# Layer 0: the dense gate's probabilities and rank comparisons moved from VectorE to GpSimd

## The reference, cut to what matters

```python
probs = softmax(x @ Wr + br, axis=-1)                 # 8 experts
sorted_idx = argsort(-probs, axis=-1)
sorted_probs = take_along_axis(probs, sorted_idx, axis=-1)
cum = cumsum(sorted_probs, axis=-1)
mask = cum < TOP_P                                    # 0.8
mask = mask.at[..., 0].set(True)
keep = take_along_axis(mask, argsort(sorted_idx), axis=-1)
gate = probs * keep
h = relu(einsum('bth,ehf->betf', x, W1) + b1)
y = einsum('betf,efh->beth', h, W2) + b2
return einsum('bte,beth->bth', gate, y)               # all eight experts are computed
```

## Time and profile before

| | |
|---|---|
| median of three runs | 2269.92 us (2262.42 to 2271.96) |
| the profiled execution's own time | 2259.05 us |
| its span, first to last instruction | 2257.3 us |
| mean granted TensorE clock | 0.955 |
| busy share of PE, DVE, ACT, POOL | 88%, 77%, 59%, 58% |
| layer 0, from its first steady iteration to its end | from about 104 us to about 1480 us |

### The profile page before, as it was taken

One profiled execution on the slowest core, in us unless ns is written; L12 is line 12 of the kernel. 1 busy time (PEld: TensorE's weight loads), 2 busy tenths in 40 slices (PEclk: granted clock), 3 DMA queues, 4 the chain that ended last, 5 costly groups with the idle time before them and its releaser, 6 DMA issues. The chain is left out here.

```text
span 2257.3 us, 40537 instructions
## 1 busy us (share of the span) xinstructions
PE 1991.2 (88%) x13714; PEld 1149.0 (51%) x13714; DVE 1730.0 (77%) x2778; ACT 1340.6 (59%) x2421; POOL 1300.4 (58%) x975
## 2 busy tenths in 40 slices
PE   1799999999999999999999999966899999987876
PEld 0455555555555555555555555533455555544442
DVE  3498888888888888888888898845777777765555
ACT  1576776776766767767767767622445554544443
POOL 0477867767767767778677687742332333324550
PEclk9999999999999999999999999967999999998897
DMA  7615505415325235145054153242222222234337
GB/s 193 137 38 111 127 26 132 102 47 130 85 63 132 68 85 132 46 107 131 22 132 104 42 131 92 46 117 88 84 91 80 85 82 86 85 109 113 114 115 230
DMA packets 184332, 222.49 MB, mean 99 GB/s; under 512 B 28488, under 2 KB 122736, under 8 KB 180016
## 3 DMA queue, kind: packets, MB, share of 16 engines
q1 hardware_dynamic: 182064, 215.52, 37.2%
q0 software_dynamic: 2048, 4.18, 0.7%
HBM read 165.41 MB, written 54.27 MB: 97 GB/s over the span
## 5 line engine op out<-in xcount | busy, mean ns | idle before, releaser
L685 POOL TENSOR_TENSOR dBx<-REP,BC 128x1024 f32<-128x1024 f32 x256 | 603.6, 2360 | 292.7 <-DVE dA L845 246.2
L845 DVE TENSOR_TENSOR_SCAN dA<-dA,dBx 128x512 f32<-128x512 f32 x512 | 626.6, 1224 | 117.4 <-ACT dA L555 66.4
L374 PE MATMUL UP<-xnT,W 128*128 128x512 f32 x1024 | 520.4, 628 | 53.9 <-ACT hT L564 41.8
L383 PEld LDWEIGHTS DN<-W,hT 128*128 128x128 f32 x4096 | 469.4, 192 | 108.6 <-issue 98.3
L383 PE MATMUL DN<-W,hT 128*128 128x128 f32 x4096 | 496.0, 278 | 0.3 <-ACT GD L571 0.3
L564 ACT ACTIVATE hT<-UP,b 128x512 f32<-128x512 f32 x512 | 355.8, 695 | 91.6 <-PE UP L374 84.4
L555 ACT ACTIVATE dA<-REP,A 128x512 f32<-128x512 f32 x512 | 354.3, 695 | 74.3 <-DVE PR L854 73.9
L854 DVE TENSOR_TENSOR PR<-dA,BC 128x512 f32<-128x512 f32 x512 | 353.4, 690 | 31.5 <-DVE dA L845 18.8
L1748 DVE TENSOR_REDUCE NM<-S 128x4 f32<-128x1024 f32 (+1 forms) x192 | 234.2, 1220 | 135.4 <-PE S L1310 88.3
L374 PEld LDWEIGHTS UP<-xnT,W 128*128 128x128 f32 x1024 | 181.6, 196 | 282.4 <-issue 146.5
L1504 ACT ACTIVATE PT<-S 128x1024 f32<-128x1024 f32 x192 | 196.8, 1025 | 111.8 <-PE S L1332 62.4
(11 more groups left out here) (246 smaller groups left out, 2819.7 us busy)
## 6 DMA issues: line engine op xcount, KB each, us to landing
REP<-s_delta SPq DMA_DIRECT2D x128, 256.0 KB, 8.2
REP<-s_dx SPq DMA_DIRECT2D x128, 256.0 KB, 7.4
BC<-s_b SPq DMA_DIRECT2D x128, 256.0 KB, 8.6
s_parts<-SPL SPq DMA_DIRECT2D x32, 384.0 KB, 2.8
s_dx<-tz SPq DMA_DIRECT2D x16, 512.0 KB, 3.1
s_y<-zeros SPq DMA_DIRECT2D x32, 256.0 KB, 5.3
YC<-s_y SPq DMA_DIRECT2D x16, 512.0 KB, 5.1
s_delta<-soft SPq DMA_DIRECT2D x32, 255.0 KB, 2.7
```

Of the source, the lines that this page charges most:

```text
L374: nc.tensor.matmul(UP[k % 2][:], W1[:, e % E0, f * P:(f + 1) * P], xnT[:, q, :], start=True, stop=True).then_inc(upf.sem, 1)
L383: last = nc.tensor.matmul(DN[:, j * P:(j + 1) * P], hT[:, e % 2, f, j * P:(j + 1) * P], W2[:, e, f, :], start=(f == 0), stop=(f == FB - 1))
L685: nc.gpsimd.tensor_tensor(dBx[:, s % 2], DX[:, h, j:j + 2, :], BC[:, q // 2, q % 2, :].unsqueeze(1).to_broadcast([P, 2, T0]), ALU.mult).th ...
L845: nc.vector.tensor_tensor_scan(h, h, dBx[:, k // 2 % 2, k % 2, :], 0.0, ALU.mult, ALU.add).then_inc(scan_done.sem, 1)
```

## The change

GpSimd makes the probabilities and the comparisons. It computes other minus this, adds tri8, which VectorE has scaled once by 2^-126 before the loop, and compares the sum with 2^-126: a positive difference passes, a zero difference passes only with the tie term. VectorE keeps the sum, the reciprocal and the two row sums. The waits on gate_step and rank_step follow.

```diff
+TINY = 2.0 ** -126
 (GpSimd, rank, h = 24)
-                pool.wait_ge(gate_step.sem, gate_step.at(n, 7))
-                nc.gpsimd.tensor_tensor(eq[:], eq[:], tri, ALU.mult).then_inc(rank_step.sem, 1)
+                this = pr[:].unsqueeze(3).to_broadcast([P, J0, E0, E0])
+                pool.wait_ge(gate_step.sem, gate_step.at(n, 4))
+                pool.wait_ge(gate_made.sem, gate_made.at(n - 1, 5))
+                nc.gpsimd.tensor_tensor(pr[:], pe_[:], g4[:, 2, :].unsqueeze(2).to_broadcast([P, J0, E0]), ALU.mult).then_inc(rank_step.sem, 1)
                 pool.wait_ge(rank_step.sem, rank_step.at(n, 1))
-                nc.gpsimd.tensor_tensor(gt[:], gt[:], eq[:], ALU.add).then_inc(rank_step.sem, 1)
+                nc.gpsimd.tensor_tensor(eq[:], other, this, ALU.subtract).then_inc(rank_step.sem, 1)
                 pool.wait_ge(rank_step.sem, rank_step.at(n, 2))
+                nc.gpsimd.tensor_tensor(eq[:], eq[:], tri, ALU.add).then_inc(rank_step.sem, 1)
+                pool.wait_ge(rank_step.sem, rank_step.at(n, 3))
+                pool.sem_inc(paced, 1)
+                nc.gpsimd.tensor_scalar(gt[:], eq[:], TINY, None, ALU.is_ge).then_inc(rank_step.sem, 1)
+                pool.wait_ge(rank_step.sem, rank_step.at(n, 4))
                 nc.gpsimd.tensor_tensor(eq[:], gt[:], other, ALU.mult).then_inc(rank_step.sem, 1)
...
 (VectorE, once before the loop)
+        nc.vector.tensor_scalar(tri8[:], tri8[:], TINY, None, ALU.mult)
...
 (VectorE, gate1, h = 22)
-                gstep(nc.vector.reciprocal(g4[:, 2, :], g4[:, 1, :]), 4)
-                dve.wait_ge(gate_made.sem, gate_made.at(n - 1, 5))
-                gstep(nc.vector.tensor_tensor(pr[:], pe_[:], over(g4[:, 2, :]), ALU.mult), 5)
-                nc.vector.tensor_tensor(gt[:], other, this, ALU.is_gt).then_inc(gate_step.sem, 1)
-                nc.vector.tensor_tensor(eq[:], other, this, ALU.is_equal).then_inc(gate_step.sem, 1)
+                nc.vector.reciprocal(g4[:, 2, :], g4[:, 1, :]).then_inc(gate_step.sem, 1)
```

More of the change, by code:

```diff
@@ L119, in layer0 @@
     sp_done = signal("sp_done", 3); relu_done = signal("relu_done", E0 * FB); da_ready = signal("da_ready", TILES); gated = signal("gated", E0)
-    conv_step = signal("conv_step", 6); gate_step = signal("gate_step", 9); lg_done = signal("lg_done", 1); gate_made = signal("gate_made", 5); z_done = signal("z_done", 2); xi_done = signal("xi_done", 1)
+    conv_step = signal("conv_step", 6); gate_step = signal("gate_step", 6); lg_done = signal("lg_done", 1); gate_made = signal("gate_made", 5); z_done = signal("z_done", 2); xi_done = signal("xi_done", 1)
     log_step = signal("log_step", 2); delta_done = signal("delta_done", 1)
@@ L126, in layer0 @@
     xn_ready = signal("xn_ready", 4); dbx_ready = signal("dbx_ready", SLOTS); yz_done = signal("yz_done", HALF); acc_done = signal("acc_done", E0)
-    dx_done = signal("dx_done", 1); rank_step = signal("rank_step", 3); r_done = signal("r_done", 1)
+    dx_done = signal("dx_done", 1); rank_step = signal("rank_step", 5); r_done = signal("r_done", 1)
     xi_loaded = signal("xi_loaded", 16); b_stored = signal("b_stored", 16); d_stored = signal("d_stored", 16 * HALF); e_stored = signal("e_stored", 16)
@@ L766, in fore @@
                 tri = tri8[:].rearrange("p (e o) -> p e o", o=E0).unsqueeze(1).to_broadcast([P, J0, E0, E0])
-                pool.wait_ge(gate_step.sem, gate_step.at(n, 7))
-                nc.gpsimd.tensor_tensor(eq[:], eq[:], tri, ALU.mult).then_inc(rank_step.sem, 1)
+                this = pr[:].unsqueeze(3).to_broadcast([P, J0, E0, E0])
+                pool.wait_ge(gate_step.sem, gate_step.at(n, 4))
+                pool.wait_ge(gate_made.sem, gate_made.at(n - 1, 5))
+                nc.gpsimd.tensor_tensor(pr[:], pe_[:], g4[:, 2, :].unsqueeze(2).to_broadcast([P, J0, E0]), ALU.mult).then_inc(rank_step.sem, 1)
                 pool.wait_ge(rank_step.sem, rank_step.at(n, 1))
-                nc.gpsimd.tensor_tensor(gt[:], gt[:], eq[:], ALU.add).then_inc(rank_step.sem, 1)
+                nc.gpsimd.tensor_tensor(eq[:], other, this, ALU.subtract).then_inc(rank_step.sem, 1)
                 pool.wait_ge(rank_step.sem, rank_step.at(n, 2))
+                nc.gpsimd.tensor_tensor(eq[:], eq[:], tri, ALU.add).then_inc(rank_step.sem, 1)
[3 more added lines that the diff above has]
+                pool.wait_ge(rank_step.sem, rank_step.at(n, 4))
                 nc.gpsimd.tensor_tensor(eq[:], gt[:], other, ALU.mult).then_inc(rank_step.sem, 1)
             if h == POOL_AT["keep"]:
-                pool.wait_ge(gate_step.sem, gate_step.at(n, 9))
+                pool.wait_ge(gate_step.sem, gate_step.at(n, 6))
                 pool.sem_inc(paced, 1)
@@ L894, in end @@
             restatistic(it)
-        def over(v, n=E0):
-            return v.unsqueeze(2).to_broadcast([P, J0, n])
         def fore(h, n, q):
@@ L902, in gstep @@
                 dve.wait_ge(gate_step.sem, gate_step.at(n, k))
-            other = pr[:].unsqueeze(2).to_broadcast([P, J0, E0, E0])
-            this = pr[:].unsqueeze(3).to_broadcast([P, J0, E0, E0])
             for b in range(HALF):
@@ L949, in fore @@
             if h == DVE_AT["gate2"]:
-                dve.wait_ge(rank_step.sem, rank_step.at(n, 3))
+                dve.wait_ge(rank_step.sem, rank_step.at(n, 5))
                 nc.vector.tensor_reduce(cnt[:], gt[:], AX.X, ALU.add).then_inc(gate_step.sem, 1)
```

## The result

The changed kernel takes 2260.24 us, the median of 20 runs (2251.89 to 2266.7), against 2269.56 for the kernel before in 20 runs of the same session. The ratio is 0.9964, with a 95% interval of 0.995 to 0.9978: 8.2 us less, within 5 to 11. The forecast was 4 us less, and 2266 for the median.

A forecast was written before the change was run, and what follows sets the result against it. Bound: a cycle from `th` through delta and dx to the B and C load, or TensorE in other iterations. VectorE 0, GpSimd's extra 0, handover -4: 2259 to 2255 us, for a median 2269.9 to 2266; range 2248 to 2280.

The forecast's parts named there:

- VectorE's 3.19 us: VectorE's time freed per iteration around the gate, near 48 us in 15, ends as shifted idle time; gain 0.
- Rival A: VectorE is on the path after all: all 48 us would give 2222, a third 2254; chance 0.13.
- GpSimd's extra 1.18 us: GpSimd's rank step grows from 2.35 to 3.53 us an iteration, with 0.77 us for the threshold; cost 0.
- The branching rule: Data-dependent branching costs GpSimd some 12 cycles an element: threshold 2.6 us, whole rank step 5.3 us.
- Rival C: GpSimd gates the next tile at dBx number 0 if its step grows over 2.7 us; 0.07 with another rival.
- The cover: GpSimd's idle time before dBx number 0, 2.7 us on average, at least 2.12, absorbs its longer rank step.
- The handover: Without VectorE's comparisons beside y and dx on GpSimd, dx ends 0.35 us earlier an iteration; 4 us in all.
- The rule on two SBUF inputs: GpSimd shares its SBUF interfaces with VectorE, in contention with instructions that have two SBUF inputs.
- rival D: VectorE's late product number 31 delays ScalarE's second dA, its relus and TensorE: at most +6, 2272; chance 0.07.
- rival B: TensorE's clock level after its convolution wait deals long and short stretches anew: 2262, or +13, about 2279; chance 0.13.

The follow-up runs named there:

- dve_one: The changed kernel with three idle row sums of one SBUF input, about 3.0 us together, on VectorE behind the reciprocal; 0.9964 of the kernel before, 2245.18 us.
- dve_two: The changed kernel with three idle products of two SBUF inputs on VectorE behind the reciprocal, where the comparisons stood; 0.9997 of the kernel before, 2250.62 us.
- after: The changed kernel itself, in its first session and profile; 0.9964 of the kernel before, 2260.24 us.
- after2: The changed kernel itself, run once more for a second profile; 0.9965 of the kernel before, 2245.43 us.
- pool_early: The changed kernel with one idle product of 128x512 on GpSimd right before dx; 1.002 of the kernel before.
- before_red: The kernel before with VectorE's two comparisons replaced by row sums of a constant tile, one SBUF input, GpSimd's three instructions kept; ratio 1.0000.
- red_late: The kernel before with row sums of a constant for the comparisons, plus one idle 128x512 product on GpSimd behind the rank step; ratio 0.9966.
- dve_less: The kernel before with VectorE's two comparisons left out and nothing in their place, GpSimd's three instructions kept; ratio 1.0017.

## Why the prediction was right, point by point

- **VectorE's 3.19 us stay idle time.** Right: its busy time falls by 49.2 us of the 48 expected, and dve_one, which puts 3.0 us an iteration back, is as fast. Rival A falls with it. The waits stand where they were expected, z0 for ScalarE and then the row sums for GpSimd, but their sizes do not hold for the iteration that the forecast was read from: 0.63 and 1.59 us, where 2.2 (3.2 less 1.0) and 0.5 were expected. In the other kind they are 2.45 and 0.42. In sum it comes to nearly the same, 1.9 and 0.8 us on average.
- **GpSimd's extra 1.18 us.** 1.26 measured. The threshold took 848 ns and not 770, the subtract 613 ns and not 730; they nearly cancel. What is left over is the extra semaphore increment, 0.20 us of idle time in place of 0.08. It is the proportional estimate that was the right one for the threshold. The branching rule of the Trainium skill (GPSIMD Engine Reference, Performance versus the Vector engine) would have made it 2.6 us if a threshold counted as such a branch; by this case's trace, with 0.85 us, it does not. Rival C falls.
- **The cover.** Right: the wait for B and C fell by 1.3 us, to 1.4. VectorE's wait in front of the first scan fell from 4.08 to 2.60 us, where about 3 was forecast.
- **The handover, the term that was mis-sized.** Its price per iteration was right: delta to dx fell by 0.19 (7.47 to 7.28) and dx itself by 0.17, and the stretches that hold no jump average 86.56 us in dve_two, and 86.17 over after, after2 and dve_one: 0.39, where 0.35 was expected. The prediction then cut it, "were it so in all 15, 5.3 ... I take 4", since TensorE waits for the convolution in 10 iterations only. dve_two less after2 is 5.2 us and less dve_one 5.4 by the medians, 7.2 and 7.4 by the ratios. That is as much as all 15 iterations give or more, but with 4 us to either side it doesn't exclude 10, and in the five stretches with a jump the profiles differ by only 0.1 us (88.14 against 88.05). pool_early says more: there the iterations with a jump pay over half of what is put in front of dx. The rule on two SBUF inputs (the Trainium skill, GPSIMD Engine Reference, Key points) agrees: two products with two such inputs bring the loss back, row sums with one do not. The price here is 0.18 us for each GpSimd instruction that starts behind one.
- **Nothing else in the change pays by itself.** dve_two holds all of the change but the handover, and is at 0.9997 (0.9986 to 1.0008), 0.8 us under the kernel before. In its set the change is worth 6.0 us by the medians and 7.9 by the ratio, in the first session 8.2, all within the intervals. The first delta starts at 70.39 us before, 68.55 after and 68.28 in after2, but at 71.39 in dve_one, which is as fast. TensorE's gaps at the jump (1.65 to 1.93 us in one profile of the change, 1.55 to 2.33 in the other) are about those before (1.57 to 2.35).
- **What the prediction did not see.** What the lateness of the rank step is good for. The prediction priced GpSimd's longer rank step at nothing because a wait covers it; between before_red (1.0000) and red_late (0.9966) this lateness is worth 0.34%. The forecast saw only that the last products come 0.8 us later, and looked for a loss in it (rival D). The two halves of the change need each other: the longer rank step with the contention still there (dve_two) gives nothing, the contention gone without the longer rank step (before_red) gives nothing, and both together give 0.36%. So it was luck that the forecast gain came: the same handover without the rank step's delay gives 1.0000, and nothing in the prediction told the two cases apart. The loads at the jump are the likely reason, and the account is not complete in size. 0.34% are 7.7 us; the profiles of before_red and red_late differ by 5.0 over the 14 stretches, of which 4.4 lie in the five with a jump, nearly all in the one of 91.88 us. dve_less, with three jumps of the kind, averages 89.41 us in those stretches, against 88.56 before.
- **The clock (rival B).** Its mechanism exists, and went the other way. The kernel before had two stretches in which TensorE fell to the lower level behind its wait for the convolution, and came 1.7 us later from there to delta; the changed kernel, whose wait is halved, had none. It is 3.4 of the 11.7 us by which layer 0 is shorter in the two profiles, but not a cause of the gain: dve_two has none of these stretches and is no faster than the kernel before. The rival's price of 13 us rested on a misreading. Of the seven long stretches five are long because they hold the loop's jump; only two could be dealt anew.

Layer 1's code is the same in both, and from the last dx to the span's end it takes 870.0 us before and 885.2 after, 871.8 in after2; no run here shows why. The spans of single profiles therefore say nothing of this change: the ratios do.

## What to carry to other kernels

When one engine hands work to another, count first which instructions of both overlapped: two SBUF operands on VectorE slowed GpSimd in front of a store that set the pace, and that was worth more than the 49 us of VectorE's time. Find the one stretch of the cycle in which a microsecond is paid in full or nearly so (here from `th` to dx) by putting an idle instruction in it, and shorten that. And if taking work away brings nothing, look for what has become early: here loads issued just ahead of a jump went with longer gaps, and making them late brought the gain back in one run and leaned that way in another.

## What the runs showed of the hardware

- A VectorE comparison or product of 128x256 with both inputs in SBUF takes 1.42 to 1.55 us beside GpSimd's instructions, and 0.42 without them; the GpSimd instruction that starts behind one is 0.18 us longer. Row sums with one SBUF input (dve_one) do not slow GpSimd (y 1.29 and dx 2.38 us beside them), and the one of 128x1024 takes 1.19 us in all 16 tiles.
- TensorE's gap at the loop's jump is 1.43 to 2.35 us at 66 jumps, and 2.64 to 3.46 at the 4 where the second group's first load was issued 0.16 us or more before the branch began. Behind the gap of 3.26 us the granted clock is 0.50, and four matmuls take 3.77 us in place of 1.98.
- GpSimd's threshold is slower than its products. One row each of the changed kernel's groups by line and shape:

```profile
L778 POOL TENSOR_SCALAR gt<-eq 128x256 f32<-128x256 f32 x16 | 13.6, 848 | 3.1 <-POOL eq L775 3.1
...
L773 POOL TENSOR_TENSOR eq<-pr 128x256 f32<-128x256 f32 x16 | 9.8, 613 | 1.2
```

The difference of two repeated views of one small tile (L773) takes 613 ns, less than the 0.73 us of a product with two full inputs.
